# Two-layer adaLN block on one core: another order for the work between layer 0 and the attention passes of layer 1

## The chip, the cores and the metric

The kernel runs on one core of one Trainium2 chip. The metric is the device time of an execution in microseconds (us). Everything is float32, and where TensorE multiplies, most operands are split in two parts (hi and lo, names ending in h and l), so that one product is three matmuls: hi x hi, hi x lo, lo x hi.

## The reference

Two layers of a transformer with modulated norms. x is (2, 512, 512): two batches of four tiles of 128 tokens.

```python
# layer 0: x -> chunked gated linear attention (32 heads), then a feed-forward ("f")
x = x + ga * L0_attn(layernorm(x) * (1 + ca) + sa)
h = layernorm(x) * (1 + cb) + sb
x = x + gb * (h @ (wscale * sign(weight) + wbias).T)
# layer 1: softmax attention ("a"), 32 query heads, 8 key heads, head size 16
h = layernorm(x) * (1 + ca) + sa
xq, xk, xv = h @ wq + bq, h @ wk + bk, h @ wv + bv      # then rope on xq and xk
x = x + ga * (softmax(q @ k.T / 4) @ v)
# then a stream-mixing layer: logits from layernorm, Sinkhorn, four streams mixed
```

The change concerns layer 0's feed-forward of batch 1 and, of layer 1, the norm h, its transposes and the projections of both batches.

## The kernel before, in words

One script, story(E), is run once for each engine. Every stage (E.ffn, E.norm and so on) is a method that each engine's class fills with its own instructions; what an engine has no part in does nothing. So the order of the calls in the script is the program order of every queue, SP's and GpSimd's too. Streams are generators of such calls; merged(a, b) interleaves two in proportion to their lengths, joined sets one behind the other.

layer0_loop ends with ffn(0) to ffn(3), the feed-forward of batch 0's tiles. Then the middle, between layer 0 and the passes (attentions), consists of:

- residual("f", i): VectorE (L1055) and GpSimd (L1679) build x after layer 0's attention for tiles 6 and 7. moments(of, i): VectorE's statistics (L1065 to L1070) and GpSimd's pow and product (L1686, L1688). norm(of, i): ScalarE writes the normalised row hh (L1422). "f" is layer 0's feed-forward, "a" layer 1's attention.
- turn_h(of, b, k): TensorE transposes a quarter of hh (L636), ScalarE writes hT2h and hF (L1435, L1436), VectorE hT2l (L1082). k runs over 0 to 3. Call these f-turns and a-turns.
- ffn(i): 12 matmuls for a tile (L644), VectorE's product with the gate (L1088), GpSimd's addition to acc (L1699), which gives the input of layer 1's norm.
- conv(part): splits and reorders the weights. Parts 0 to 7 are the query weights (ScalarE L1455, VectorE L1097), 8 the key weights (VectorE L1101, L1104), 9 the value weights. When part 7 is done the event v_aw("q") fires.
- memsets(b), key_ones(b): GpSimd fills vp and ksT (L1707, L1763). key_ones(0) waits for v_aw("q"), since ksT lies where the raw query weights lay. bias(0): GpSimd copies the biases to abp in eight copies (L1738, L1741). bias(1): TensorE's six small transposes of them (L676), which wait for those copies.
- proj(b, u): 24 matmuls (L695). u = 2 is the keys, 0 and 1 are the two groups of queries. prod_u and comb: VectorE's and GpSimd's rope products and sums (L1131, L1751, L1753). vproj(b): the values (L712, L714), copied by ScalarE (L1477). high, low: the split parts hl (ScalarE L1490, VectorE L1152); the first high also waits for ffn(7), on whose weights hl lies. place_u: SP stores hl to scratch in DRAM (k_scr, q_scr; L1913 to L1933), waits until it has landed, and loads it in another layout into ksT and qsT (L1922, L1940).

The script before: merged(second_front, merged(starts(0), weights2)), that is batch 1's residuals, f-norms, f-turns and ffn 4 to 7, interleaved with batch 0's a-norms and a-turns and with the convs; then merged(parts(0), starts(1)), with the projections of batch 0 and the a-norms and a-turns of batch 1; then parts(1). bank() deals out PSUM banks 0, 1, 2 in turn; the unit's results use the banks unit_banks, vproj bank 6.

Behind it SP loads the constants and modulation rows of the passes (r_loads, load_mods). pass_a (L730) finds the row maxima; max_part writes them by a DMA into qsT (L1962, qsT<-mT), and only then the scores of the passes begin (L751).

Of the kernel before, what the change touches and what calls it, by code (L numbers as in the profile page):

```python
# [9 lines left out]
ACTF = mybir.ActivationFunctionType  # L10
# [59 lines left out]
def build(nc, I, out, cst_w):  # L70
# [3 lines left out]
    def sig(name, step=1):  # L74
        return Sig(ctx.enter_context(nc.semaphore(name)), step)
# [16 lines left out]
    banks = [pairs[i // 2][:, i % 2 * 512:i % 2 * 512 + 512] for i in range(8)]  # L92
# [84 lines left out]
    def over(kb, name, shape, dt=F32, end=None):  # L177
        place[0] = base_h + int(kb * 1024)
        t = sb(name, shape, dt)
        assert end is None or place[0] <= base_h + end * 1024, name  # L180
        return t
# [35 lines left out]
    vps = [over(96, "vp0", [128, 4, 8, 32]), over(116, "vp1", [128, 4, 8, 32])]  # L217
# [10 lines left out]
    for b in range(2):  # L228
# [59 lines left out]
    a_fT, a_hh, a_n, a_qkv, a_aw, a_part, a_pt, a_mT, a_exp, a_oS = [sig(n) for n in  # L288
        ("a_fT", "a_hh", "a_n", "a_qkv", "a_aw", "a_part", "a_pt", "a_mT", "a_exp", "a_oS")]
# [22 lines left out]
            plan.append(weights.pop(0))  # L312
    assert not weights
    src_of = {"q": "wq", "g": "wg", "k": "wk", "v": "wv", "o": "wo"}
    pbank = (0, 1, 2)
    bS, bY, bC, bT, bO = 3, 4, 5, 6, 7

    ln_of = {"f": (0, 4, 3), "a": (1, 1, 0)}
# [26 lines left out]
    def key_cols(ap):  # L345
        return ap.rearrange("p (g c h r) -> p h r g c", g=2, h=2, r=8)

    unit_banks = ((0, 1), (2, 3), (4, 5))

    def unit_buf(b, u):  # L350

# [17 lines left out]
    class Stages:  # L369


        def __init__(self, e):
            self.e = e
            self.sent = self.nsplit = self.nproj = self.nmod = self.npa = self.nspin = 0
            self.drain = {}
            self.ready = {}
            self.done = {}
            self.ropes, self.vswap = [], {}
            self.mod_at, self.prod_free, self.turned = {}, {}, []
# [10 lines left out]

        def bank(self):
            self.nproj += 1
            return pbank[(self.nproj - 1) % 3]

        def swap(self, key):

# [62 lines left out]
    class Tensor(Stages):  # L459
# [240 lines left out]
        def vproj(self, b):  # L700
            pe = self.e
            if b == 0:
                pe.wait_ge(*v_aw("v"))
                pe.wait_ge(*d_a[2]("rows"))
                pe.wait_ge(*g_vp("two"))
            pe.wait_ge(*self.drain[6])
            for j in range(4):
                o, sl = banks[6][:, j * 128:(j + 1) * 128], slice(j * 128, (j + 1) * 128)
                c = 0
                for k in range(4):  # L710
                    for x_, w_ in ((hT2h, vwh), (hT2h, vwl), (hT2l, vwh)):
                        pe.matmul(o, x_[b][:, k, sl], w_[:, k, :], start=(c == 0), stop=False)  # L712
                        c += 1
                mm = pe.matmul(o, one2[:, :], brow[:, :], start=False, stop=True)  # L714
            mm.then_inc(*p_qkv.up("v", b))
            self.drain[6] = a_qkv("v", b)


        def pass_a(self, b, p, i):
# [568 lines left out]
    class Scalar(Stages):  # L1288
# [184 lines left out]
        def vproj(self, b):  # L1473
            ac = self.e
            ac.wait_ge(*p_qkv("v", b))
            ac.wait_ge(*g_vp("one", b))
            ac.activation(vps[b][:, :, :, 0:16], banks[6].rearrange("p (j h d) -> p j h d", j=4, h=8), ACTF.Copy).then_inc(*a_qkv.up("v", b))  # L1477

        def high(self, b, u):
            ac, (z_, n_) = self.e, unit_buf(b, u)  # L1480
# [510 lines left out]
    def stream(E, make, *a):  # L1991
        return Stream(make(E, *a), sum(1 for _ in make(Stages(None), *a)))
# [8 lines left out]
    def merged(a, b):  # L2001

        na, nb = a.left, b.left

        def steps():
            k = 0
            for i in range(na):
                a.step()
                yield
                while k * na < (i + 1) * nb and k < nb:  # L2010
                    b.step()
                    k += 1
                    yield
            while b.step():
                yield
        return Stream(steps(), na + nb)

    def joined(*parts):
        def steps():
            for p in parts:  # L2020
                while p.step():
                    yield
        return Stream(steps(), sum(p.left for p in parts))
# [18 lines left out]
    def residuals(E, of, tiles):  # L2042
        for i in tiles:
            E.residual(of, i), (yield)

    def norms(E, of, b):
        i0 = 4 * b
        for i in range(i0, i0 + 6):
            if i < i0 + 4:
                E.moments(of, i), (yield)  # L2050
            if i >= i0 + 2:
                E.norm(of, i - 2), (yield)

    def turns(E, of, b):
        for k in range(4):
            E.turn_h(of, b, k, E.bank(), *E.spare((of, b, k))), (yield)

    def ffns(E, tiles):
        for i in tiles:
            E.ffn(i, E.bank()), (yield)  # L2060
# [14 lines left out]
        E.tables(2, E.bank()), E.tables(3, E.bank()), (yield)  # L2075
        yield from turns(E, "f", 0)

    def second_front(E):
        yield from residuals(E, "f", (6, 7))
        yield from norms(E, "f", 1)  # L2080
        yield from turns(E, "f", 1)
        yield from ffns(E, range(4, 8))

    def starts(E, b):
        yield from norms(E, "a", b)
        yield from turns(E, "a", b)

    def weights2(E):
        for part in (8, 9, 0, 1, 2, 3, 4, 5, 6, 7):
            E.conv(part), (yield)  # L2090
            if part == 9:
                E.memsets(0), (yield)
            if part == 2:
                E.bias(0, None), (yield)
            if part == 5:
                E.bias(1, E.bank()), (yield)
        E.memsets(1), E.key_ones(0), (yield)

    def parts(E, b):
        k, g0, g1 = 2, 0, 1  # L2100
        if b:
            E.key_ones(1)
        E.proj(b, k), (yield)
        E.proj(b, g0), (yield)
        E.prod_u(b, k), (yield)
        E.comb(b, k), (yield)
        E.vproj(b), (yield)
        E.prod_u(b, g0), (yield)
        E.high(b, k), E.low(b, k), E.place_u(b, k), (yield)
        E.comb(b, g0), (yield)  # L2110
        E.proj(b, g1), (yield)
        E.prod_u(b, g1), (yield)
        E.high(b, g0), E.low(b, g0), E.place_u(b, g0), (yield)
        E.comb(b, g1), (yield)
        E.high(b, g1), E.low(b, g1), E.place_u(b, g1), (yield)
# [105 lines left out]
    def layer0_head(E):  # L2221
        E.load_consts()
        E.silu()
        for i in range(4):
            E.load_x(i)
        E.x_stats(0)
        E.mod_head()
        for i in range(4, 8):
            E.load_x(i)
        E.mod_bcast()  # L2230
        E.load_tabs()
        for _ in range(NRAW):
            E.send("act")
        E.x_stats(1)
        E.h_rows(0)
        E.h_rows(1)
        for i in range(NT):
            if i + 2 < NT:
                E.h_rows(i + 2)
            E.h_turn(i)  # L2240
            if i >= 4:
                E.split()
        E.win_split()
        E.win(0)
        E.win(1)
        E.z_turn()
        ahead = stream(E, first_pieces)
        for part in range(8):
            E.gate(part)
            if part < 7:  # L2250
                ahead.step(), ahead.step()
        for b in range(2):
            E.gsum(b)
            ahead.step(), ahead.step()
        E.gtot(0)
        ahead.step(), ahead.step()
        E.gtot(1)
        ahead.rest()
        E.loop_start()
# [100 lines left out]
    def story(E):  # L2360
        layer0_head(E)
        layer0_loop(E)
        merged(stream(E, second_front), merged(stream(E, starts, 0), stream(E, weights2))).rest()
        merged(stream(E, parts, 0), stream(E, starts, 1)).rest()
        stream(E, parts, 1).rest()
        E.r_loads()
        E.load_mods()
        pending = joined(stream(E, head, 0), stream(E, mixes, 0))
        attentions(E, pending)
        pending.rest()  # L2370
        stream(E, head, 1).rest()
        E.mix_y(1)
        merged(stream(E, sinkhorn), joined(stream(E, branch, 0), stream(E, branch, 1))).rest()
        stream(E, finish).rest()
        E.end()

    for cls in (Scalar, Sync, Tensor, Vector, Pool):
        story(cls(Idle()))
# [3 lines left out]
    @block.sync  # L2382
    def _(e):
        story(Sync(e))

    @block.tensor
    def _(e):
        story(Tensor(e))
# [74 lines left out]
```

## Time and profile before

| | us |
|---|---|
| median of 3 runs | 1644.7 (1642.51 to 1648.16) |
| profiled execution | 1641.26 |
| its span | 1639.5 |

Busy over the span: TensorE 77%, VectorE 62%, GpSimd 46%, ScalarE 39%. The page cuts the span in 40 slices of 41 us. TensorE is at nine tenths or more in most slices of layer 0 and between 3 and 9 in slices 25 to 30 (984 to 1230 us), which hold the end of layer 0 and the stretch that is edited. In these slices the granted clock (PEclk, in tenths of 2.4 GHz) falls too.

```profile
PE   2768999999999999999999997659638998940000
PEclk8889999999999999999999999768858999965555
DMA  5121112122122121121122202201891000000001
```

To read it: each digit is one slice, the first row TensorE's busy share in tenths, the third that of the 16 DMA engines. In two slices (29 and 30) the DMA engines have 8 and 9 tenths, more than anywhere else; there TensorE falls to 6 and 3.

### The profile page before, as it was taken

Reading aid. Unit: us, or ns where it says so; the run is one execution under the profiler, and the core shown is the slowest. Engines: PE = TensorE matmul, PEld = TensorE weight load, DVE = VectorE, ACT = ScalarE, POOL = GpSimd, SP = SyncE. Lnnn points to the kernel's source line nnn. Section 1 sums busy time; section 2 is a strip of 40 time slices with the busy share of each in tenths; the row PEclk is TensorE's granted clock in tenths of the full one; section 3 lists DMA queues with packets and bytes.
Section 4 is the critical chain, followed back from the end, with each engine's and each line's share of the span. In section 5 each row is a group of like instructions: output and inputs, shape, how many; then the busy total and the mean of one; then the engine's idle time right before and its main releaser. Section 6 shows DMA issues by size and latency. Waiting matters only on the chain. (4 is left out here: it accounts for less than half of the span.)

```text
span 1639.5 us, 18558 instructions
## 1 busy us (share of the span) xinstructions
PE 1264.2 (77%) x6071; PEld 894.2 (55%) x6071; DVE 1020.0 (62%) x1700; ACT 633.4 (39%) x1198; POOL 756.8 (46%) x742
## 2 busy tenths in 40 slices
PE   2768999999999999999999997659638998940000
PEld 0557776767767768767767775548513334320000
DVE  4644665655565565656556556553446888448898
ACT  0323333433433433334334232352106777733323
POOL 2336656656755756665757565643200012041017
PEclk8889999999999999999999999768858999965555
DMA  5121112122122121121122202201891000000001
GB/s 173 52 61 40 52 56 87 52 71 71 52 78 67 55 72 59 52 65 52 52 71 59 66 12 83 85 1 32 142 154 50 2 2 2 2 1 0 0 0 52
DMA packets 71136, 87.53 MB, mean 53 GB/s; under 512 B 6921, under 2 KB 40873, under 8 KB 70466
## 3 DMA queue, kind: packets, MB, share of 16 engines
q1 hardware_dynamic: 69170, 83.63, 19.3%
q10 hardware_dynamic: 1872, 2.72, 0.4%
q8 instruction: 50, 0.82, 0.2%
q14 instruction: 44, 0.36, 0.1%
HBM read 78.54 MB, written 7.52 MB: 52 GB/s over the span
## 5 line engine op out<-in xcount | busy, mean ns | idle before, releaser
L1161 DVE TENSOR_REDUCE nm<-banks 128x2 f32<-128x1024 f32 x128 | 152.1, 1220 | 50.2 <-PE banks L730 49.5
L1626 POOL TENSOR_TENSOR sw<-sw,sinT 128x512 f32<-128x512 f32 x80 | 103.1, 1289 | 141.6 <-ACT sw L1354 141.6
L1403 ACT ACTIVATE yTh<-yF 128x512 fp32r<-128x512 f32 x64 | 40.4, 632 | 324.3 <-DVE yF L1018 324.3
L1638 POOL TENSOR_TENSOR dec<-gb,gcol 128x512 f32<-128x512 f32 x64 | 70.3, 1099 | 202.4 <-DVE Sd L984 194.7
L1509 ACT ACTIVATE Pb<-banks 128x512 f32<-128x512 f32 x256 | 134.8, 601 | 73.6 <-PE banks L751 73.2
L583 PE MATMUL banks<-st,qt 128*128 128x128 f32 x384 | 82.2, 299 | 52.7 <-DVE Sd L984 27.6
L531 PE MATMUL banks<-hTh,wgh 128*128 128x512 f32 x256 | 121.6, 475 | 0.0
L751 PE MATMUL banks<-qsT,ksT 50*128 50x512 f32 x256 | 90.4, 488 | 36.0 <-DMA qsT<-mT 27.1
L956 DVE SCALAR_TENSOR_TENSOR gs<-tg,banks 128x512 f32<-128x512 f32 x64 | 44.0, 687 | 119.1 <-ACT tg L1361 119.1
L531 PE MATMUL banks<-hTh,wqh 128*128 128x512 f32 x256 | 107.9, 422 | 0.0
L1681 POOL TENSOR_TENSOR acc<-acc,hh 128x512 f32<-128x512 f32 x8 | 10.5, 1315 | 207.3 <-DVE hh L1060 207.3
L611 PE MATMUL banks<-woh,yTh 128*128 128x512 f32 x256 | 103.5, 404 | 0.5 <-DVE yTl L1021 0.5
L584 PE MATMUL banks<-xc,Sd 128*128 128x128 f32 x512 | 97.7, 290 | 4.9 <-DVE Sd L984 4.9
L531 PE MATMUL banks<-hTh,wql 128*128 128x512 f32 x256 | 101.4, 396 | 0.0
L611 PE MATMUL banks<-woh,yTl 128*128 128x512 f32 x256 | 101.0, 395 | 0.0
L531 PE MATMUL banks<-hTl,wqh 128*128 128x512 f32 x256 | 100.7, 394 | 0.0
L611 PE MATMUL banks<-wol,yTh 128*128 128x512 f32 x256 | 100.5, 393 | 0.0
L531 PE MATMUL banks<-hTl,wgh 128*128 128x512 f32 x256 | 100.4, 392 | 0.0
L531 PE MATMUL banks<-hTh,wgl 128*128 128x512 f32 x256 | 100.3, 392 | 0.0
L583 PEld LDWEIGHTS banks<-st,qt 128*128 128x128 f32 x384 | 66.0, 208 | 62.2 <-DVE Sd L984 37.5
L1021 DVE TENSOR_TENSOR yTl<-yF,yTh 128x512 fp32r<-128x512 f32 x64 | 69.8, 1090 | 45.4 <-ACT yTh L1403 45.4
L751 PEld LDWEIGHTS banks<-qsT,ksT 50*128 50x128 f32 x256 | 36.7, 189 | 104.8 <-ACT Pb L1509 39.1
(303 smaller groups left out, 3470.0 us busy)
## 6 DMA issues: line engine op xcount, KB each, us to landing
gb<-g_scr SPq DMA_DIRECT2D x64, 256.0 KB, 3.5
raw<-in_wmod SPq DMA_DIRECT2D x40, 256.0 KB, 2.7
raw<-in_wo SPq DMA_DIRECT2D x32, 256.0 KB, 2.9
raw<-in_wq SPq DMA_DIRECT2D x31, 256.0 KB, 2.7
raw<-in_wg SPq DMA_DIRECT2D x31, 256.0 KB, 2.7
qsT<-q_scr SPq DMA_DIRECT2D x24, 256.0 KB, 9.0
q_scr<-hl SPq DMA_DIRECT2D x32, 128.0 KB, 8.0
mt<-mods_scr SPq DMA_DIRECT2D x12, 256.0 KB, 11.3
```

What stands on the lines that cost most here:

```text
L531: mm = pe.matmul(banks[bk][:, :], w_[:, k, :], x_[:, k, b * 512:(b + 1) * 512], start=(c == 0), stop=(c == 11))
L583: pe.matmul(o, qt[:, h, :], st[:, h, :], start=True, stop=False)
L584: mm = pe.matmul(o, Sd[:, h, :], xc[:, h, :], start=(n == 0), stop=True)
L611: mm = pe.matmul(banks[bO][:, :], y_[:, h, :], w_[:, :], start=(c == 0), stop=(c == 11))
L751: pe.matmul(banks[bk], k_[64 * g:64 * g + 50, p // 4, kt * 128:(kt + 1) * 128], q_[64 * g:64 * g + 50, p % 8, :], start=True, stop=True).t ...
L956: ve.scalar_tensor_tensor(out=gs[t % 2][:, n, :], in0=tg[:, :], scalar=1.0, in1=banks[bk][:, :], op0=ALU.add, op1=ALU.mult).then_inc(*v_ga ...
L1021: ve.tensor_tensor(yTl[:, :, :], yF[:, :, :], yTh[:, :, :].bitcast(F32), ALU.subtract).then_inc(*v_yl.up(s))
L1161: ve.tensor_reduce(nm[:, b, i, p:32:16], pairs[z_][:, :].rearrange("p (g t) -> p g t", g=2), AX.X, ALU.max, negate=True).then_inc(*v_nm.up ...
L1403: ac.activation(yTh[:, :, :], yF[:, :, :], ACTF.Copy).then_inc(*a_yh.up(s))
L1509: ac.activation(Pb[kt % 2][:, 2 * g + pr, :], banks[bk], ACTF.Exp, scale=0.25).then_inc(*a_exp.up(b, qd, kt, pr, g))
L1626: po.tensor_tensor(s_[:, :], s_[:, :], sinT[:, :], ALU.mult).then_inc(*g_rope.up("sin", kind, t, n))
L1638: po.tensor_tensor(dec[:, :, :], gb[s % 2][:, :, :], bc(gcol[:, t % 2, heads(t), n], 2, 128), ALU.subtract).then_inc(*g_dec.up("sub", s))
```

## The change

The middle is written out as one list of calls, middle(E). Batch 0's moments and norms of "a" come first, its a-turns before batch 1's f-turns, proj(0, 2) before the f-turns and proj(0, 0) before ffn(4). memsets and key_ones(0) come in front of bias(0, None). The ffn tiles 5 to 7, batch 1's a-norms and a-turns are merged with the rest of parts(0). From the middle on, bank() deals out banks 2, 6, 7; the query units use banks 0, 1 and 4, 5, the key unit 4, 5, and vproj bank 3.

```diff
--- before.py
+++ after.py
@@ -312,7 +312,7 @@
             plan.append(weights.pop(0))
     assert not weights
     src_of = {"q": "wq", "g": "wg", "k": "wk", "v": "wv", "o": "wo"}
-    pbank = (0, 1, 2)
+    pbank, mbank = (0, 1, 2), (2, 6, 7)
     bS, bY, bC, bT, bO = 3, 4, 5, 6, 7
 
     ln_of = {"f": (0, 4, 3), "a": (1, 1, 0)}
@@ -345,7 +345,7 @@
     def key_cols(ap):
         return ap.rearrange("p (g c h r) -> p h r g c", g=2, h=2, r=8)
 
-    unit_banks = ((0, 1), (2, 3), (4, 5))
+    unit_banks = ((0, 1), (4, 5), (4, 5))
 
     def unit_buf(b, u):
 
@@ -373,6 +373,7 @@
             self.e = e
             self.sent = self.nsplit = self.nproj = self.nmod = self.npa = self.nspin = 0
             self.drain = {}
+            self.late = False
             self.ready = {}
             self.done = {}
             self.ropes, self.vswap = [], {}
@@ -390,7 +391,7 @@
 
         def bank(self):
             self.nproj += 1
-            return pbank[(self.nproj - 1) % 3]
+            return (mbank if self.late else pbank)[(self.nproj - 1) % 3]
 
         def swap(self, key):
 
@@ -703,9 +704,9 @@
                 pe.wait_ge(*v_aw("v"))
                 pe.wait_ge(*d_a[2]("rows"))
                 pe.wait_ge(*g_vp("two"))
-            pe.wait_ge(*self.drain[6])
+            pe.wait_ge(*self.drain[3])
             for j in range(4):
-                o, sl = banks[6][:, j * 128:(j + 1) * 128], slice(j * 128, (j + 1) * 128)
+                o, sl = banks[3][:, j * 128:(j + 1) * 128], slice(j * 128, (j + 1) * 128)
                 c = 0
                 for k in range(4):
                     for x_, w_ in ((hT2h, vwh), (hT2h, vwl), (hT2l, vwh)):
@@ -713,7 +714,7 @@
                         c += 1
                 mm = pe.matmul(o, one2[:, :], brow[:, :], start=False, stop=True)
             mm.then_inc(*p_qkv.up("v", b))
-            self.drain[6] = a_qkv("v", b)
+            self.drain[3] = a_qkv("v", b)
 
 
         def pass_a(self, b, p, i):
@@ -1474,7 +1475,7 @@
             ac = self.e
             ac.wait_ge(*p_qkv("v", b))
             ac.wait_ge(*g_vp("one", b))
-            ac.activation(vps[b][:, :, :, 0:16], banks[6].rearrange("p (j h d) -> p j h d", j=4, h=8), ACTF.Copy).then_inc(*a_qkv.up("v", b))
+            ac.activation(vps[b][:, :, :, 0:16], banks[3].rearrange("p (j h d) -> p j h d", j=4, h=8), ACTF.Copy).then_inc(*a_qkv.up("v", b))
 
         def high(self, b, u):
             ac, (z_, n_) = self.e, unit_buf(b, u)
@@ -2075,33 +2076,44 @@
         E.tables(2, E.bank()), E.tables(3, E.bank()), (yield)
         yield from turns(E, "f", 0)
 
-    def second_front(E):
-        yield from residuals(E, "f", (6, 7))
-        yield from norms(E, "f", 1)
-        yield from turns(E, "f", 1)
-        yield from ffns(E, range(4, 8))
-
     def starts(E, b):
         yield from norms(E, "a", b)
         yield from turns(E, "a", b)
 
-    def weights2(E):
-        for part in (8, 9, 0, 1, 2, 3, 4, 5, 6, 7):
-            E.conv(part), (yield)
-            if part == 9:
-                E.memsets(0), (yield)
-            if part == 2:
-                E.bias(0, None), (yield)
-            if part == 5:
-                E.bias(1, E.bank()), (yield)
-        E.memsets(1), E.key_ones(0), (yield)
+    def middle(E):
+
+        E.late = True
+        E.conv(8), E.conv(9)
+        E.moments("a", 0), E.residual("f", 6)
+        E.moments("a", 1), E.norm("a", 0)
+        E.residual("f", 7)
+        for i in (2, 3):
+            E.moments("a", i), E.norm("a", i - 1)
+        E.moments("f", 4), E.norm("a", 3)
+        E.conv(0), E.moments("f", 5), E.norm("f", 4)
+        for k in range(4):
+            E.turn_h("a", 0, k, E.bank(), *E.spare(("a", 0, k)))
+            if k < 2:
+                E.moments("f", 6 + k), E.norm("f", 5 + k)
+            E.conv(k + 1)
+        E.norm("f", 7)
+        E.memsets(0), E.memsets(1), E.key_ones(0)
+        E.bias(0, None)
+        E.proj(0, 2)
+        for k in range(4):
+            E.turn_h("f", 1, k, E.bank(), *E.spare(("f", 1, k)))
+            if k < 3:
+                E.conv(k + 5)
+        E.bias(1, E.bank())
+        E.proj(0, 0)
+        E.ffn(4, E.bank())
 
     def parts(E, b):
         k, g0, g1 = 2, 0, 1
         if b:
             E.key_ones(1)
-        E.proj(b, k), (yield)
-        E.proj(b, g0), (yield)
+            E.proj(b, k), (yield)
+            E.proj(b, g0), (yield)
         E.prod_u(b, k), (yield)
         E.comb(b, k), (yield)
         E.vproj(b), (yield)
@@ -2360,8 +2372,8 @@
     def story(E):
         layer0_head(E)
         layer0_loop(E)
-        merged(stream(E, second_front), merged(stream(E, starts, 0), stream(E, weights2))).rest()
-        merged(stream(E, parts, 0), stream(E, starts, 1)).rest()
+        middle(E)
+        merged(joined(stream(E, ffns, range(5, 8)), stream(E, starts, 1)), stream(E, parts, 0)).rest()
         stream(E, parts, 1).rest()
         E.r_loads()
         E.load_mods()
```

## Rows read from the trace of the kernel before

**Rows 1.** Timeline, TensorE: start, us, line, tile, count, [idle before <- releaser].
```profile
1091.81 2.82 PE L636 MATMUL banks<-cst,hh 128*128 128x128 f32 x12 [15.13 <-ACT hh L1422]
```

**Rows 2.** Chain of waits: start us, us, what, from 1100 to 1236.
```profile
1102.29 8.44 PE banks L644 x24
...
1117.15 11.05 PE banks L695 x48
...
1134.14 2.75 PE banks L712 x12
...
1137.30 8.06 PE banks L695 x24
...
1154.78 13.44 PE banks L695 x48
...
1173.24 1.49 PE banks L712 x12
...
1176.98 11.91 DMA k_scr<-hl
...
1224.18 11.15 DMA qsT<-mT
```

**Rows 3.** Timeline, SP's queue, the first scratch stores and loads.
```profile
1139.17 0.35 SPq L1913 DMA_DIRECT2D k_scr<-hl  x1
...
1141.96 2.63 SPq L1922 DMA_DIRECT2D ksT<-k_scr  x6
...
1149.16 2.42 SPq L1928 DMA_DIRECT2D q_scr<-hl  x4
```

**Rows 4.** Stretches of 20 us: busy per engine, PEclk, DMA share, GB/s.
```profile
1140.00:1160.00 20.00, 13.42 (x49) 10.58 (x48) 8.61 (x12) 8.20 (x13) 4.72 (x3) 0.69 0.75 147
...
1160.00:1180.00 20.00, 20.00 (x110) 16.94 (x109) 7.14 (x10) 2.15 (x4) 2.55 (x2) 1.00 1.02 157
```

**Rows 5.** Timeline, VectorE, 1078 to 1084.
```profile
1078.99 0.68 DVE L1101 TENSOR_TENSOR kwl<-kp,kwh 128x512 fp32r<-128x512 f32 x1
...
1081.33 0.68 DVE L1055 TENSOR_TENSOR acc<-acc,mt 128x512 f32<-128x512 f32 x1
...
1082.53 0.68 DVE L1065 BATCH_NORM_STATS2 bst<-acc 128x6 f32<-128x512 f32 x1
...
1083.60 0.68 DVE L1065 BATCH_NORM_STATS2 bst<-acc 128x6 f32<-128x512 f32 x1
```

**Rows 6.** Timeline, GpSimd, 1079 to 1121.
```profile
1079.08 1.71 POOL L1679 TENSOR_TENSOR acc<-acc,xin 128x512 f32<-128x512 f32 x1
...
1086.80 0.55 POOL L1686 TENSOR_TENSOR rs<-ve,neghalf 128x1 f32<-128x1 f32 x1
...
1092.13 1.70 POOL L1738 COPY abp<-ab 1x128 f32<-1x128 f32 x4
...
1093.79 1.49 POOL L1741 COPY abp<-ab 1x64 f32<-1x64 f32 x4
...
1120.48 1.81 POOL L1763 MEMSET ksT<- 128x2048 f32 x1
```

**Rows 7.** Timeline, ScalarE, 1087 to 1149.
```profile
1087.65 1.52 ACT L1422 ACTIVATE hh<-acc,nmr,rs 128x512 f32<-128x512 f32 x2 [1.18 <-POOL nmr L1688]
...
1094.30 0.64 ACT L1455 ACTIVATE aqh<-aqr 128x256 fp32r<-128x256 f32 x1
...
1094.83 0.77 ACT L1435 ACTIVATE hT2h<-banks,colv 128x512 fp32r<-128x512 f32 x1
...
1148.50 1.16 ACT L1490 ACTIVATE hl<-pq 128x512 fp32r<-128x512 f32 x2
```

**Rows 8.** Stretches of 4 us around the first stores.
```profile
1132.00:1136.00 4.00, 4.00 (x19) 3.77 (x19) 0.00 (x0) 0.00 (x0) 0.00 (x0) 0.50 0.00 0
...
1148.00:1152.00 4.00, 1.96 (x8) 1.57 (x8) 4.00 (x7) 2.46 (x5) 2.55 (x2) 0.63 0.38 88
...
1152.00:1156.00 4.00, 1.23 (x4) 1.03 (x4) 3.93 (x6) 3.01 (x5) 2.17 (x2) 0.50 0.61 142
```

## The prediction, before the change was run

> **What bounds the kernel now.** I read the page's slices first, then busy time by stretch, the chain of waits, and the timelines of each engine between the end of layer 0 (about 1076 us) and the first scored tile of the passes (1235 us). Layer 0 before and the passes behind are not edited. The stretch holds three stages.
>
> First, TensorE stands idle for 15.1 us: the last ffn tile of batch 0 ends at 1076.7, and the next transposes wait for ScalarE's normalised rows hh of batch 1 [rows 1]. Second, a dense stretch runs from 1102.3 to 1137.3: ffn tiles, proj(0,2), proj(0,0) and vproj(0), with proj(0,1) right behind [rows 2]. The end of vproj(0), call it V = 1137.3, releases ScalarE's copy of the values and behind it hl of the keys, so SP's first scratch store goes out at 1139.17, 1.9 us after V [rows 3]. Third, from there to 1235.3 the DMA queue is the bound: share 0.75 and then 1.02 in the two stretches shown [rows 4], and the chain goes through k_scr (11.9 us) and ends in qsT<-mT, which lands at 1224.2 + 11.15 = 1235.3 [rows 2]. V to the passes is 98.0 us. What counts is (a) how far V moves and (b) what changes in the 98 us behind it.
>
> **The change: the start of the middle.** All matmuls stay; only the order and the banks change. V still comes after all eight transposes, proj(0,2), proj(0,0), four ffn tiles and vproj(0), since ffn 5 to 7 stand ahead of vproj in the merged order (and hl waits for ffn 7). So V can only gain idle time or clock.
>
> VectorE begins at 1077.3. It now does conv 8 (2.34, from 1078.99 to 1081.33 before), conv 9 (0.6), four moments of 1.07 (1082.53 to 1083.60) and two residuals of 0.6: 2.34 + 0.6 + 4.28 + 1.2 = 8.4, so 1085.7 [rows 5]. GpSimd follows with two additions of 1.7 and a pow with its product (0.75, of which the row's 0.55 is the pow) for each tile [rows 6]: the fourth a-tile is through at 1087.7, and its norm on ScalarE (0.76 of the pair's 1.52) at 1088.4 [rows 7]. Each a-turn takes two activations on ScalarE, whose rows of 0.77 overlap so that they start 0.66 apart: 1.32; conv k+1 takes 0.53 (1094.30 to 1094.83) [rows 7]; norms 4 to 6 of batch 1 and conv 0 lie between. Sum on ScalarE from 1088.4: conv 0 0.5, norm f4 0.7, four turns 5.3, three convs 1.6, norms f5 and f6 1.4, and small waits for the conv and moments that alternate on VectorE, about 0.8: 1098.7. VectorE's last hT2l is at 1099.4. So proj(0,2) starts at 1099.4, where the old dense stretch started at 1102.3: only 2.9 us gained, since that old stretch already had its transposes behind it.
>
> proj(0,2) has 24 matmuls. The 24 that opened the old stretch took 8.44, the 48 at full clock 11.05 (5.5 for 24) [rows 2]. I take 8.4: 1107.8. Then come the f-turns, with conv 5, 6 and 7 between them on ScalarE: 0.6 + 3 x (1.32 + 0.53) = 6.2, so 1114.0, and VectorE's half of conv 7 is done at 1114.7.
>
> **The added wait.** In the new order GpSimd has key_ones(0) ahead of bias(0). key_ones(0) waits for v_aw("q"), which is conv 7. Before, GpSimd's bias copies ran at 1092.1, well ahead of key_ones at 1120.5 [rows 6]. Now: conv 7 is done at 1114.7, key_ones 1.8, the eight bias copies 1.7 + 1.5 = 3.2, so 1119.7. On TensorE bias(1), six tiny transposes of those copies (0.7), stands ahead of proj(0,0), and behind it all four ffn tiles and vproj. So proj(0,0) starts at 1120.4. TensorE has then been idle, but for the f-turns, since 1107.8. Without key_ones it could start at 1114.7, where conv 7 frees it too; the wait alone costs 5.7.
>
> From 1120.4: proj(0,0) behind a long pause. The 48 matmuls that opened behind the pause at 1154.8 took 13.44 against 11.05 [rows 2], so 5.5 + 2.4 = 7.9. Four ffn tiles: 48 matmuls, 11.1. vproj: its quarter is 1.49 at full clock (plus 0.25 for the row's matmul) and was 2.75 plus 0.4 in the slow part [rows 2], so 6.9 at full clock; it took 9.1 in the old place. V = 1120.4 + 7.9 + 11.1 + 6.9 = 1146.3, or 1148.5 with the slow vproj. Against 1137.3: **+9.0 to +11.2**. The same in parts: the start gives back 2.9, the f-turns with conv 5 to 7 now stand open between the projections (6.9) and the wait adds 5.7; the old stretch lasted 35.0 and its work now takes 34.3 to 36.5.
>
> What the clock does here is unknown. The row of 1132 to 1136 shows TensorE fully busy at a granted 0.50 [rows 8], that is 1.2 GHz, although it had worked without a gap since 1102. The Trainium skill (TensorE: Matmul & The Clock Gate, part 1) says that activity releases the throttle and an idle engine falls back to it. By that rule the dense vproj would have stayed at 2.4 GHz, and my sum would take +9.0; the row speaks against the rule here and would give +11.2. The sum itself goes by the rows at both levels, nearer the fast one, since most of the stretch was at it: +9.7.
>
> **What is saved behind V.** The merged order puts high_g0 ahead of batch 1's turns, and the units use banks 4 and 5, so that a turn no longer waits for a product. ScalarE after V: the copy 0.5, like the other plain copies, hl(k) 0.6 (half of its 1.16 for two) [rows 7], four norms 2.8 (the last one waits for its moments), hl(g0) 1.2: 5.4. So the keys go out at V + 1.2 and the first query stores at V + 6.7, behind SP's six ksT issues (2.6, which wait for the key stores to land, 2.8 after the first one went out). Before, they went at 1149.16 = V + 11.9 [rows 3]. The hole that this fills is visible: 1148 to 1156 shows DMA shares of 0.38 and 0.61 [rows 8], that is 4 x (0.62 + 0.39) = 4.0 us unused. proj(1,2) starts at V + 14.2 instead of V + 17.5 (1154.8): proj(0,1) 5.6, then four turns, hl(g1) and the last hT2l. vproj(1) ends 3.3 earlier, so batch 1's key store (1177.0, V + 39.7) is at V + 36.4, where queue and TensorE arrive together again. As the queue is the bound, I credit its hole and not the producers' lead: **-4.0**. Bounds: 0, if the hole only moves to the next wait for a landing, and -5.2, the whole lead of the first query stores.
>
> The passes themselves and the table of banks (vproj on 3, mbank 2, 6, 7) I cost at 0: each reused bank has its reader done by then (a ScalarE pair of 1.32 against three banks in turn). If that cover failed, a turn would wait at most for one VectorE tile, 0.7. The row DMA of the biases and one2 are early and hidden.
>
> **Sum.** +9.7 - 4.0 = +5.7 us. The profiled execution was 1641.3 (span 1639.5), so 1647.0; the median of the three runs is 1644.7, 3.4 above the profiled one, and I give the forecast against it: 1644.7 + 5.7 = **1650.4 us**.
>
> **Rivals.**
> 1. *Full clock, a wash.* TensorE's first pause ends 3 us sooner, so proj(0,2) may run at 2.4 GHz (5.5 instead of 8.4), proj(0,0) as well (5.5 instead of 7.9) and vproj at 6.9. Then V = 1146.3 - 2.9 - 2.4 = 1141.0, +3.7, and with -4.0 to -5.2 the total is -0.3 to -1.5: 1643.2 to 1644.4. For it: at 1160 to 1180 all is at 1.00 [rows 4]. Against it: at 1102.3 and at 1154.8 the clock was low behind pauses of this size [rows 2].
> 2. *Faster.* The bias copies do not bind, because conv 7 finishes early enough, and the DMA stage pulls in the whole 5.2. Place: conv 5 to 7 on ScalarE, while proj(0,2) runs. It would need them finished before 1108.9 (then GpSimd is done by 1113.9); proj(0,0) starts at 1114.7 or before, V at 1137.7 at full clock or earlier, and with -5.2 the total is -4.8 or better: about 1639 if they were done when proj(0,2) ends. Against it: ScalarE and VectorE take them in program order behind the f-turns, which wait for TensorE. It decides for faster only where V stays at 1137.3 or below.
> 3. *The lead behind V is lost.* The queue is full anyway, and the hole turns up elsewhere (SP stands still for each landing, as for k_scr's 11.9). Then +9.7 stays: 1654.4, and 1655.9 with the slow vproj.
>
> **How the numbers follow.** Forecast (+3.5 to +7.5) 0.45; lost lead, +7.5 and more, 0.15; full clock, -4 to +3.5, 0.30; faster 0.10. What this kernel's measurement can tell from no change is 0.3%, 4.9 us. The forecast's case lies partly inside it: 0.35 of its 0.45 beyond +4.9. Slower by more than 0.3%: 0.35 + 0.15 = 0.50. Within: 0.10 + 0.30 = 0.40. Faster: 0.10. The range leaves out one in ten on either side: 1641.0 (the faster case) to 1656.0 (lost lead with the slow vproj).
>
> **What would show it.** Right: GpSimd's L1763 memset waits on VectorE's L1097 (aql) and its bias copies end within 2 us of 1120; TensorE's first matmul of L695 is near 1099 and it has a second idle time of 6 to 10 us ahead of bias(1), L676; V near 1146; query stores under 8 us behind V; the first L751 near 1241. Wrong: bias copies before 1110; V at or ahead of 1137; a DMA queue with as large a hole as before; or a move of more than 3 us outside this stretch.

## The result, and the profile after

The changed kernel takes 1652.4 us (median of 8 runs, 1649.9 to 1659.3) against 1641.7 for the kernel before (8 runs, 1635.6 to 1648.8): ratio 1.0062, 95% interval 1.0037 to 1.0087. The profiled execution has a span of 1657.5 us, 18.0 more than the one before, which is more than the medians moved: single executions of this kernel differ by several us, and much of what follows is about taking that apart.

The slices of the page: as before, with TensorE low in slices 25 to 30.

```profile
PE   2778999999999999999999996748628999940000
...
PEclk8879999999999999999999998778858999955555
...
DMA  4121112122122121121122203100991000000001
```

Four marks cut the program so that profiles can be compared whatever happened in layer 0: F, the end of ffn(3); V, the end of vproj(0); S, the first matmul of the scores (L751 before, L752 after); and the last matmul of the scores. In the profile before F is 1076.7, in the one after 1083.5: 6.8 us of the 18.0 arose in layer 0, which is not edited. F to S went from 158.7 to 164.6, +5.9. S to the last score went from 202.9 to 206.4, and from there to the branch's first transpose from 40.4 to 42.3; the rest is 160.8 and 160.7. (In the changed kernel's three further profiles the 42.3 is 40.4.) So in this one pair 12 us arose outside the edited stretch, which the prediction names as a sign of being wrong (a move of more than 3 us there); e9 to e12 below ask whether it belongs to the change.

TensorE between F and V (timeline: start, us, line, [idle before <- releaser]):

```profile
1095.57 3.77 PE L637 MATMUL banks<-cst,hh 128*128 128x128 f32 x16 [12.11 <-ACT hh L1423]
...
1106.85 0.80 PE L696 MATMUL banks<-hT2h,kwh 128*128 128x512 f32 x1 [7.51 <-DVE hT2l L1083]
...
1116.69 0.66 PE L637 MATMUL banks<-cst,hh 128*128 128x128 f32 x4 [0.66 <-ACT hF L1437]
...
1125.76 0.80 PE L677 MATMUL banks<-cst,abp 1*128 1x1 f32 x6 [8.41 <-POOL abp L1742]
```

The 15.1 us pause [rows 1] is now 12.1, proj(0,2) (L696) starts 23.4 us behind F, and there is a new pause of 8.4 us ahead of bias(1), L677. What it waits for stands on GpSimd:

```profile
1121.65 1.81 POOL L1764 MEMSET ksT<- 128x2048 f32 x1 [14.37 <-DVE aql L1098]
...
1123.41 1.39 POOL L1739 COPY abp<-ab 1x128 f32<-1x128 f32 x4
...
1124.75 0.96 POOL L1742 COPY abp<-ab 1x64 f32<-1x64 f32 x4
```

The reader should see the bracket of the first row: GpSimd has been idle for 14.4 us until VectorE's aql, which is conv 7. The memset is key_ones(0); in the kernel before, the copies stood ahead of it and were done at 1095.3 [rows 6]. The chain of waits of the changed kernel runs through just these rows:

```profile
1106.85 7.87 PE banks L696 x24
...
1121.65 1.81 POOL ksT L1764
...
1126.56 8.27 PE banks L696 x24
...
1134.82 10.90 PE banks L645 x48
...
1150.74 1.49 PE banks L713 x12
...
1167.96 13.68 PE banks L696 x48
...
1190.40 9.90 DMA k_scr<-hl
...
1235.91 12.16 DMA qsT<-mT
```

It has GpSimd's ksT and then 48 matmuls of ffn (10.9) and vproj's quarters at 1.49. [Rows 2] had 2.75 for the last quarter: in this profile vproj runs at full clock, 1.00 in the stretch from 1148 shown below. V is at 1152.5. Behind it on SP's queue:

```profile
1153.66 0.35 SPq L1914 DMA_DIRECT2D k_scr<-hl  x1
...
1157.34 2.63 SPq L1923 DMA_DIRECT2D ksT<-k_scr  x6
...
1160.02 2.42 SPq L1929 DMA_DIRECT2D q_scr<-hl  x4
```

The keys go out at V + 1.2 and the first query stores at V + 7.5, where they went at V + 11.9 [rows 3]. The hole of [rows 8] lay from 11 to 19 us behind V, at DMA shares of 0.38 and 0.61. In the changed kernel the share is 0.72 and 0.93 from 4 us behind V on, and 1.01 and 1.13 where the hole was (stretches of 4 us: busy per engine, PEclk, DMA share, GB/s).

```profile
1148.00:1152.00 4.00, 4.00 (x33) 3.72 (x32) 3.93 (x9) 0.00 (x0) 1.54 (x5) 1.00 0.00 0
...
1156.00:1160.00 4.00, 3.68 (x22) 2.81 (x20) 2.64 (x7) 2.72 (x5) 2.01 (x4) 1.00 0.72 164
...
1160.00:1164.00 4.00, 0.66 (x4) 0.42 (x4) 3.87 (x5) 2.44 (x4) 3.29 (x3) 0.83 0.93 116
...
1164.00:1168.00 4.00, 0.04 (x1) 0.04 (x1) 2.59 (x4) 3.19 (x6) 0.59 (x1) 0.50 1.01 314
1168.00:1172.00 4.00, 4.00 (x10) 3.13 (x11) 0.00 (x0) 0.00 (x0) 0.00 (x0) 0.50 1.13 131
```

The gain behind V shows in the landing of batch 1's key store (k_scr<-hl in the chain): at 1176.98 + 11.91, that is V + 51.6, before [rows 2], and at 1190.40 + 9.90, V + 47.8, here. From that landing to S it is 46.5 and 47.8 us.

### The profile page after: what moved, and what is told of

It is laid out like the page before. It is cut to its first block and busy times, and to the rows that moved or that the text cites. A ratio compares the mean times of both kernels' runs of the same rounds, so it can differ in the third digit from the quotient of the medians.

```text
span 1657.5 us, 18558 instructions
## 1 busy us (share of the span) xinstructions
PE 1274.8 (77%) x6071; PEld 898.4 (54%) x6071; DVE 1024.8 (62%) x1700; ACT 633.5 (38%) x1198; POOL 756.7 (46%) x742
## 5 line engine op out<-in xcount | busy, mean ns | idle before, releaser
L1639 POOL TENSOR_TENSOR dec<-gb,gcol 128x512 f32<-128x512 f32 x64 | 70.4, 1100 | 206.5 <-DVE Sd L985 199.1
L1404 ACT ACTIVATE yTh<-yF 128x512 fp32r<-128x512 f32 x64 | 40.4, 632 | 324.4 <-DVE yF L1019 324.4
L752 PE MATMUL banks<-qsT,ksT 50*128 50x512 f32 x256 | 92.9, 501 | 35.2 <-DMA qsT<-mT 28.4
L1682 POOL TENSOR_TENSOR acc<-acc,hh 128x512 f32<-128x512 f32 x8 | 10.5, 1318 | 210.1 <-DVE hh L1061 210.1
L584 PEld LDWEIGHTS banks<-st,qt 128*128 128x128 f32 x384 | 67.4, 213 | 62.3 <-DVE Sd L985 37.5
L752 PEld LDWEIGHTS banks<-qsT,ksT 50*128 50x128 f32 x256 | 37.6, 194 | 105.3 <-ACT Pb L1510 38.1
```

Source lines behind the costliest of these rows:

```text
L584: pe.matmul(o, qt[:, h, :], st[:, h, :], start=True, stop=False)
L752: pe.matmul(banks[bk], k_[64 * g:64 * g + 50, p // 4, kt * 128:(kt + 1) * 128], q_[64 * g:64 * g + 50, p % 8, :], start=True, stop=True).t ...
L1639: po.tensor_tensor(dec[:, :, :], gb[s % 2][:, :, :], bc(gcol[:, t % 2, heads(t), n], 2, 128), ALU.subtract).then_inc(*g_dec.up("sub", s))
```

## The experiments

e1 to e8 were each timed in 5 rounds beside the kernel before. All marks, from one profile each, in us:

| kernel | F to V | V to S | F to S | scores | ratio to before (95%) |
|---|---|---|---|---|---|
| before | 60.6 | 98.1 | 158.7 | 202.9 | |
| before, e9 | 57.8 | 98.9 | 156.7 | 204.6 | |
| before, e10 | 60.6 | 99.4 | 160.0 | 206.8 | |
| changed | 69.0 | 95.6 | 164.6 | 206.4 | 1.0062 (1.0037 to 1.0087) |
| changed, e1 | 68.2 | 93.5 | 161.7 | 206.9 | 1.0046 (1.0019 to 1.0072) |
| changed, e11 | 69.1 | 93.3 | 162.4 | 208.4 | |
| changed, e12 | 68.2 | 95.1 | 163.3 | 204.4 | |
| e2 bias first | 65.0 | 96.1 | 161.1 | 204.0 | 1.0008 (0.9987 to 1.0030) |
| e3 old front | 60.6 | 95.7 | 156.3 | 203.9 | 0.9995 (0.9972 to 1.0018) |
| e4 old back | 69.1 | 95.5 | 164.5 | 208.2 | 1.0055 (1.0037 to 1.0073) |
| e5 convs ahead | 61.3 | 95.8 | 157.1 | 210.1 | 0.9990 (0.9972 to 1.0008) |
| e6 before, mods late | 57.7 | 93.5 | 151.2 | 203.8 | 0.9965 (0.9947 to 0.9984) |
| e7 short chain | 54.7 | 95.5 | 150.1 | 206.3 | 0.9952 (0.9931 to 0.9973) |
| e8 short chain, mods late | 54.7 | 91.2 | 145.9 | 206.0 | 0.9953 (0.9929 to 0.9977) |

**The changed kernel again.**

> The changed kernel again, beside the kernel before on one chip. My theory: the stretch between layer 0 and the first scored tile is 6.0 us longer (V, the end of vproj(0), +8.4 after the last ffn tile of the loop; V to the first scored tile -2.4), and what the whole time shows beyond that is granted clock in stretches that were not edited. So +6 us over before, and a profile in which the passes' length is within 1 us of before's whenever the clock is the same. Rival: something behind the passes' start is systematically slower as well, +10 us again, with the extra 4 to 5 us again in the passes and the head behind them.

Measured: 1649.3 against 1644.3, +4.9 by the medians and +7.6 by the ratio. F to S is 161.7, 3.0 above the one profile of before and not 6.0; the rival's +10 did not come again. The extra 4 us in the scores is there again (206.9), but a single profile of before was too little to compare it with; see e9 to e12.

**e2, the bias copies first.**

```diff
-        E.memsets(0), E.memsets(1), E.key_ones(0)
         E.bias(0, None)
+        E.memsets(0), E.memsets(1), E.key_ones(0)
```

> One edit on the changed kernel: GpSimd's bias copies go ahead of the memsets and key_ones(0). Theory (the wait for conv 7 through key_ones holds TensorE): proj(0,0) starts when conv 7 is done, 121.65 on the clock where it started at 126.5, so 4.8 us less than the changed kernel, of which all arrives at the passes since the queue's work behind V only slides. Rival (the DMA queue is what bounds, the wait was covered): no change. Second rival (the pause of TensorE is shorter, so the clock is full in proj(0,0)): up to 7 us less.

Measured: 1644.3, equal to before and 5.0 below the changed kernel measured beside it. F to V fell by 3.6 against the mean of the changed kernel's four (68.6). TensorE:

```profile
1110.09 0.50 PE L677 MATMUL banks<-cst,abp 1*128 1x1 f32 x6 [1.31 <-ACT hF L1437]
...
1113.13 0.77 PE L696 MATMUL banks<-hT2h,aqh 128*128 128x512 f32 x1 [2.54 <-DVE hT2l L1083]
```

bias(1) now waits 1.3 us instead of 8.4, but proj(0,0) stands 2.5 us longer, for conv 7. (The bracket names hT2l; the last VectorE work ahead of 1113.13 is conv 7's aql, 1112.45 + 0.58.) GpSimd's memset, no longer in front of anything:

```profile
1113.09 1.81 POOL L1764 MEMSET ksT<- 128x2048 f32 x1 [11.79 <-DVE aql L1098]
```

So proj(0,0) starts 39.1 us behind F where it started at 43.0, and V moves with it: the order of memset and copies cost about 4 us up to V, where 4.8 was expected. That all of it reaches the passes this run doesn't show by itself: F to S is 161.1, only 1.9 below the changed kernel's mean (163.0), and the intervals of the two ratios overlap. e5 settles it. The second rival falls: proj(0,0) took 7.8 us, not 5.5.

**e5, convs 5 to 7 ahead.**

```diff
+        for part in (5, 6, 7):
+            E.conv(part)
         E.memsets(0), E.memsets(1), E.key_ones(0)
         E.bias(0, None)
...
             E.turn_h("f", 1, k, E.bank(), *E.spare(("f", 1, k)))
-            if k < 3:
-                E.conv(k + 5)
```

> The changed kernel, with conv 5, 6 and 7 issued ahead of proj(0,2) instead of between the f-turns; key_ones(0) stays ahead of the bias copies. Theory: what holds TensorE is conv 7 standing behind turns that wait for proj(0,2). With it early, key_ones and the copies are done while proj(0,2) runs, TensorE's pause ahead of bias(1) (8.4 us) falls to under 1 us and V is 8 to 9 us sooner than in the changed kernel: 2 to 3 below the kernel before. Rival (the order key_ones, then bias is what costs, as the run with the bias copies first would have it): 4 to 5 us. Rival (covered by the queue): 0.

Measured: ratio 0.9990, F to V 61.3, that is 7.3 below the changed kernel. key_ones is still ahead of the copies, but now all are done 4.4 us before TensorE comes to them:

```profile
1101.30 1.80 POOL L1764 MEMSET ksT<- 128x2048 f32 x1 [2.35 <-DVE aql L1098]
...
1104.43 0.97 POOL L1742 COPY abp<-ab 1x64 f32<-1x64 f32 x4
```

```profile
1109.81 0.50 PE L677 MATMUL banks<-cst,abp 1*128 1x1 f32 x6 [0.77 <-ACT hF L1437]
```

The ratio lies clear of the changed kernel's (1.0019 to 1.0072), and F to S is 157.1, 5.9 below its mean: the rival of a wait that the queue covers falls. The order on GpSimd costs only because conv 7, for which key_ones waits, stood behind turns that wait for a projection. With conv 7 early the copies are in time although key_ones is ahead of them, and proj(0,0) itself, which needs conv 7's weights and still waited for them in e2, is free too; so e5 gains 3.7 more at V than e2. Expected were 8 to 9. The pause is gone as expected and proj(0,0), no longer behind a pause, took 5.9 us instead of 8.3, but vproj(0) took 9.6 instead of 6.9: the mean granted clock in it was 0.69.

**e3 and e4, meant as the two halves of the change.** e3 has the front of before, proj(0,2) and proj(0,0), then starts(1) merged with parts(0), and the changed kernel's banks; e4 has the changed front and banks, then ffn 5 to 7 and the merged call of before:

```diff
-        merged(joined(stream(E, ffns, range(5, 8)), stream(E, starts, 1)), stream(E, parts, 0)).rest()
+        stream(E, ffns, range(5, 8)).rest()
+        merged(stream(E, parts, 0), stream(E, starts, 1)).rest()
```

> The front of the kernel before (its order up to ffn 7 and the convs), then proj(0,2) and proj(0,0), then the changed kernel's merged order and banks behind it. Theory: V as before, and V to the first scored tile shorter by the filled hole of the DMA queue, 2.4 us: -2 to -3 us against before. Rival a (the producers' lead counts, not the hole): -5. Rival b (the queue finds the same holes later): 0.

> The changed kernel's front and banks, but ffn 5 to 7 first and then the merged order of before: parts(0) interleaved with batch 1's norms and turns, high of the first queries behind two turns. Theory: V to the first scored tile goes back towards 98 us, so +2.4 us over the changed kernel (8 to 9 over before). Rival (the -2.4 came from the banks, not from the order): same as the changed kernel.

Measured: e3 0.9995, within noise; its profile has F to V as before and V to S 95.7, 3.1 below the mean of the three of before (98.8). The times alone can't tell -2 from 0. e4: 1.0055, V to S 95.5, not back at 98. But e4 doesn't bring the old order back, against what its expectation says. In the kernel before, parts(0) began with the two projections, which are now in middle(E); with them gone, merged() deals its calls out otherwise, and the high of the first queries stands behind one turn. It stood behind two before and stands behind none in the changed kernel. e3 has this same halfway order behind V. SP's queue of e3, with V at 1136.5, and of e4, with V at 1145.6:

```profile
1138.42 0.36 SPq L1914 DMA_DIRECT2D k_scr<-hl  x1
...
1147.12 2.42 SPq L1929 DMA_DIRECT2D q_scr<-hl  x4
```

```profile
1147.47 0.36 SPq L1914 DMA_DIRECT2D k_scr<-hl  x1
...
1154.56 2.42 SPq L1929 DMA_DIRECT2D q_scr<-hl  x4
```

The queries go out at V + 10.6 and V + 9.0, against V + 11.9 before, and V to S is the same 95 to 96 in both. Common to both are the new banks and half of the new order. In the kernel before, the last two turns waited for VectorE's product pq in their bank:

```profile
1150.04 1.97 PE L636 MATMUL banks<-cst,hh 128*128 128x128 f32 x8 [3.81 <-DVE pq L1131]
```

In e3 the last turn waits 0.67 us for ScalarE:

```profile
1146.62 0.66 PE L637 MATMUL banks<-cst,hh 128*128 128x128 f32 x4 [0.67 <-ACT hF L1437]
...
1153.43 0.79 PE L696 MATMUL banks<-hT2h,kwh 128*128 128x512 f32 x1 [6.16 <-DVE hT2l L1083]
```

The landing of batch 1's key store tells more than V to S. Chains of e3, of e4 and of the changed kernel in e1 (V at 1147.0):

```profile
1177.32 8.33 DMA k_scr<-hl
```

```profile
1184.27 10.44 DMA k_scr<-hl
```

```profile
1187.48 7.09 DMA k_scr<-hl
```

It lands at V + 49.1 in e3 and in e4. In the four profiles with the order and banks of before (e6 among them) it lands at V + 51.2 to 51.6, in the changed kernel's four at V + 47.0 to 47.8, and in e2, e5, e7 and e8, whose order behind V is the changed kernel's, at V + 48.0 to 48.4. So banks and half of the order give about 2.3 us, and the other half of the order 0.7 to 2.1 more. No run has the banks without the order, so what the banks give alone is not shown.

**e6 and e8, the modulation rows behind the start of the passes.**

```diff
         E.r_loads()
-        E.load_mods()
...
+            if Q == 2:
+                E.load_mods()
             if Q == 4:
                 E.gates()
```

> The kernel before with one edit: load_mods (8 loads of 256 KB that the head behind the passes needs) is issued at Q == 2 of the passes instead of ahead of them. Theory (the DMA queue bounds V to the first scored tile, and the row maxima's qsT<-mT lands behind these 2 MB): V to the first scored tile falls from 98 by the 3.7 us of issues and some 8 to 10 us of transfer, 10 to 13 us in all, and the whole time by as much, 1632 to 1634. Rival (TensorE or VectorE bounds that stretch, through the row maxima): under 4 us. Rival (the loads then collide with the row maxima's DMAs of the passes): gained and given back, 0.

Measured: 0.9965, -6 us. V to S is 93.5, 5.3 below the mean of before, not 10 to 13. The chain of e6, and the landing of the last load ahead of the modulation rows (rwt: count, KB each, us from issue to landing) in the kernel before, issued at 1219.10, and in e6, issued at 1217.38:

```profile
1176.55 10.99 DMA k_scr<-hl
...
1218.66 11.11 DMA qsT<-mT
```

```profile
rwt<-in_rw SPq DMA_DIRECT2D x1, 48.0 KB, 11.4
```

```profile
rwt<-in_rw SPq DMA_DIRECT2D x1, 48.0 KB, 12.3
```

So rwt lands at 1230.5 before and at 1229.7 in e6, 93.2 and 93.5 us behind V. In e6 qsT<-mT lands with it, at 1229.8; in the kernel before it lands at 1235.3 [rows 2], 4.8 us behind it, and these 4.8 us are the 2 MB, the last of which lands at 1235.2:

```profile
1230.00:1234.00 4.00, 0.00 (x0) 0.00 (x0) 0.00 (x0) 0.00 (x0) 0.00 (x0) 0.50 1.05 405
```

The row is of the kernel before: 405 GB/s, against 147 and 157 in the scratch traffic of [rows 4]. So the modulation rows take the queue about half of the time that was expected of them. The 3.7 us that SP needs to issue them don't add to it, since the loads ahead of them are still under way. qsT<-mT takes 11.1 us from issue to landing in both kernels because it is issued 5.5 us sooner in e6 and lands 5.6 us sooner; that it is the same figure says nothing about what stands ahead of it. Not all that e6's profile is shorter by from F to S is its edit: F to V is 57.7 with the front untouched, as in e9, since the granted clock in vproj(0) was 0.96 there.

**e7, a version made from these.** conv 8 and 9 behind the a-moments, f-norms and convs behind the a-turns, the copies first:

```diff
-        E.conv(8), E.conv(9)
         E.moments("a", 0), E.residual("f", 6)
...
+        E.norm("a", 3)
+        E.conv(8), E.conv(9)
+        E.moments("f", 4)
+        E.bias(0, None)
         for k in range(4):
             E.turn_h("a", 0, k, E.bank(), *E.spare(("a", 0, k)))
-            if k < 2:
-                E.moments("f", 6 + k), E.norm("f", 5 + k)
-            E.conv(k + 1)
+            if k < 3:
+                E.moments("f", 5 + k)
+        for i in range(4, 8):
+            E.norm("f", i)
+        for part in range(8):
+            E.conv(part)
         E.memsets(0), E.memsets(1), E.key_ones(0)
-        E.bias(0, None)
         E.proj(0, 2)
...
-            if k < 3:
-                E.conv(k + 5)
```

> The changed kernel with its middle rewritten: conv 8 and 9 behind the four a-moments, the f-norms and conv 0 to 7 behind the a-turns, so that they run beside proj(0,2), and the bias copies ahead of the memsets and key_ones. Theory (V moves with the chain of waits on TensorE): proj(0,2) starts 3 us sooner for conv 8 and 9 and 4 to 5 sooner for the a-turns' chain, and the 8 us pause ahead of bias(1) is gone: V minus the end of ffn(3) 53 to 55 where it was 69 in the changed kernel and 60.6 before, the total 6 to 8 below before. Rival (the queue behind V takes the lead back): same as before.

Measured: 1635.7 against 1643.0, ratio 0.9952. F to V is 54.7, as forecast:

```profile
1085.44 2.82 PE L637 MATMUL banks<-cst,hh 128*128 128x128 f32 x12 [9.40 <-ACT hh L1423]
...
1095.66 0.80 PE L696 MATMUL banks<-hT2h,kwh 128*128 128x512 f32 x1 [6.32 <-DVE hT2l L1083]
...
1106.37 0.50 PE L677 MATMUL banks<-cst,abp 1*128 1x1 f32 x6 [0.77 <-ACT hF L1437]
```

The three pauses are 9.4, 6.3 and 0.8 us, where the changed kernel had 12.1, 7.5 and 8.4. The sum came out as forecast by other terms: proj(0,2) starts 19.6 us behind F, 3.8 sooner and not 7 to 8, and proj(0,0), with no long pause ahead of it, took 5.9 us instead of 8.3, which the expectation had not counted.

> Both edits: the rewritten middle and load_mods at Q == 2. Theory: the two gains add up, since one moves V and the other shortens what follows it: 16 to 20 us below before, about 1626. Rival (with V earlier something else bounds the passes' start, the products or the row maxima on VectorE): 10 to 12 below.

Measured: 1633.1, ratio 0.9953, that is 8 to 10 below before and not 16 to 20. F to S is the shortest of all, 145.9, and V to S is 4.3 below e7's, about what e6 gained; yet the ratio is that of e7 and the medians are 2.5 apart. Whether the late loads cost the passes something, or the noise hides 4 us, stays open. e7 and e8 beat both kernels.

**e9 to e12, is the rest slower too?**

> The kernel before, for another profile of its passes (first to last matmul of the scores). So far they last 202.9 to 203.9 us in the three kernels with the old front and 204.0 to 210.1 in the seven with the new one. Theory (which stretches of the passes run at a low granted clock varies from run to run): the kernel before shows 206 or more in one of two further profiles, and its length follows the stretches with a clock under 0.95. Rival (the new order makes the passes longer): 203 again, both times.

> As the run before it, a second time: by the theory of the varying clock anything from 203 to 210, by the rival 203.

> The changed kernel again, for its passes: by the theory of the varying clock anything from 203 to 210 us, by the rival 206 to 207 as in its first two profiles. The stretch from the end of ffn(3) to the first scored tile: 161.7 to 164.6 as so far, against 158.7 in the kernel before.

> As the run before it, a second time: 203 to 210 us, or 206 to 207.

Measured (spans 1636.6, 1640.1, 1648.0 and 1648.7): the scores took 204.6 and 206.8 in the kernel before, 208.4 and 204.4 in the changed one. Both have short and long ones. The whole of the scores in the shortest profile, that of the kernel before, and in the longest, e5:

```profile
1235.37:1438.27 202.90, 189.14 (x1143) 78.63 (x1143) 155.56 (x226) 153.01 (x302) 15.36 (x20) 0.97 0.01 2
```

```profile
1232.22:1442.32 210.10, 198.23 (x1143) 81.61 (x1143) 155.61 (x226) 152.96 (x302) 15.33 (x20) 0.92 0.01 2
```

VectorE (third number behind the stretch's length) and ScalarE (fourth) are busy for the same time in both; TensorE is busy for 9 us longer, and its mean granted clock (third number from the end) is 0.92 against 0.97. Over all fourteen profiles the length goes with this clock: it is 0.95 to 0.97 in the six profiles of 205 us or less and 0.92 to 0.95 in the eight longer ones. How often the clock dips in the passes differs between profiles of one kernel (0.97, 0.95 and 0.94 in the three of before).

Whether the new order makes the dips more frequent is not settled. The mean length is 204.8 in the three of before and 206.5 in the changed kernel's four, inside their spread. With the experiments taken in, it is 204.4 in the five profiles with the old front and 206.7 in the nine with the new one. But the same pooling gives F, the end of a layer 0 that is the same in all of them, 2.2 us later in the nine. A systematic part of 2 us isn't excluded.

## Why the prediction came out right

The forecast was 1650.4 (range 1641.0 to 1656.0) and 5.7 us slower. Measured were 1652.4 and +10.7 in the first comparison, with an interval from 6 to 14, and +4.9 in e1. That the first time comes so near the forecast is in part luck: the base of 1644.7, a median of three, was 3.0 us above the median of eight (1641.7). By the marks, mean of three profiles of before and four of after, F to S grew by 163.0 - 158.5 = 4.5, and the mechanism that the prediction names is the one that e2 and e5 take away.

- *The start.* Forecast: transposes 11.7 us behind F, proj(0,2) at 22.7. Measured 12.1 and 23.4.
- *The added wait.* Conv 7 and key_ones' start at 38.0 forecast, 38.2 measured (37.5 in two of the four profiles); proj(0,0) at 43.7 forecast, 43.0 measured (42.3 in the same two). The term that is off is the copies, 3.2 forecast from [rows 6], 2.3 measured. e2 and e5 showed the wait to be on the path; against e2 the order alone is worth about 4 us, not 5.7.
- *V.* Forecast at 69.6 to 71.8 behind F, +9.0 to +11.2 against a V of 60.6, and taken at +9.7; measured 68.6 in the mean of four, and the profile of before with 60.6 is one of two such, the third has 57.8. So the mean moved by 68.6 - 59.7 = +8.9. Both ends lie about 1 us below the forecast's (68.6 instead of 69.6, 59.7 instead of 60.6), and that they cancel is chance. The clock did not sort the two kernels: the mean granted clock in vproj(0) was 0.71, 0.90 and 0.72 in the profiles of before, and 1.00, 0.95, 1.00 and 0.94 in those of the changed kernel.
- *Behind V.* -4.0 forecast; 94.4 - 98.8 = -4.4. The size was right and so is the filled hole, but the way there is only partly the forecast's. The first query stores left at V + 7.2 to 7.5, not 6.7, since the key stores took 3.7 us to land and not 2.8. proj(1,2) came at V + 15.5 and 16.7, not 14.2, and batch 1's key store left at V + 37.9 to 40.4, not 36.4; it landed at V + 47.0 to 47.8 all the same, whether it left early or late, as it must if the queue ahead of it is the bound. How the gain divides between order and banks, which the forecast put down to the order, is open (e3, e4).
- *The rest of the time.* The sum left layer 0 and the passes at 0. Against the one profile of before, those of the two kernels moved by -4.5 to +6.8 us in layer 0 and by up to +5.5 in the passes, as much as the whole effect. The medians leave 6 us of the first comparison's +10.7 that F to S doesn't account for, and 0.4 of e1's +4.9; by e1's ratio it would be 3. This is not explained beyond that spread.
- *The rivals.* The wash at full clock did not come: proj(0,2) and proj(0,0) took 7.9 and 8.3 us (7.2 and 7.9 in e1 and e12), at the low clock first. The lost lead did not come either, and conv 7 was not early. e5 made that true by hand and took V nearly back to before (61.3), with a ratio of 0.9990: no loss any more, but not rival 2's gain of 4.8 us, since V to S shrank by 3.0 and not by 5.2. By its own terms that rival's V is 1114.7 + 5.5 + 11.1 + 6.9 = 1138.2, not 1137.7, and its gain 4.3.

## What to carry to other kernels

Before moving a block ahead, list what each engine's queue has in front of it: one memset that waits for a late event held eight small copies, and these held TensorE. Of its pause of 8.4 us this order cost about 4 (e2), and most of the rest was the late event itself (e5). Where the same work stays ahead of the mark (here V), a reordering can change only idle time and clock, so count the pauses on both sides and look for links that make engines wait in turn (projection, turn, conv, memset, copy, projection). When you test order against another edit, write out the order that results: here the script's interleaving moved a call that the edit did not name, and e4 was no longer the test it was meant to be. Behind a full queue look at landings and not at issues: two DMAs that both took 11.1 us landed 5.6 us apart. Compare profiles by marks and not by spans, and take several: F to S of one kernel varied by 3 us, its span by 9.5.

## What the runs showed of the hardware

The granted clock fell to 0.50, that is 1.2 GHz, inside vproj(0) of the kernel before, with TensorE busy without a gap since 1102: 5.3 us ahead of V in two of its three profiles and 1.6 us ahead in the third, which had V 2.8 us sooner with the same instructions. Of the changed kernel's four, two kept 2.4 GHz through vproj and two lost it 0.8 to 0.9 us ahead of V. The stretch of vproj(0) in e9, where V was sooner, and in e1:

```profile
1124.36:1131.91 7.55, 7.55 (x54) 6.89 (x52) 2.07 (x3) 0.00 (x0) 2.54 (x2) 0.90 0.00 0
```

```profile
1139.86:1147.04 7.18, 7.18 (x54) 6.52 (x52) 6.77 (x18) 0.00 (x0) 2.81 (x6) 0.95 0.00 0
```

By the rule of the Trainium skill (TensorE: Matmul & The Clock Gate, part 1), that activity releases the throttle, none of these dense stretches would lose the clock. The traces agree in two of these seven profiles; in the others the clock falls without a pause, and this has to be allowed for.

Eight copies on one partition took 2.3 us on GpSimd where VectorE and ScalarE did nothing beside them (the changed kernel, e5) and 3.2 to 3.5 where both were at work (before, e2, e7). A small DMA landed when the 2 MB issued ahead of it had landed, 4.8 us later than without them (e6).
